# Audio-tower kernel on one Trainium2 core: one-hots by broadcast operands, small products moved around the token product, and five unused products in the prologue

## Chip, cores and metric

The kernel runs on one core of one Trainium2 chip. Time is device microseconds of one execution of the whole program, lower is better. The profile is of one execution; its times start at the first instruction.

## What is computed

Three layers over an input of 32 sequences of 125 frames with 23 features.

```python
# 1. token layer: windows of 5 frames, a product, relu, batch norm over all 32*121 rows
y = relu(einsum('blf,of->blo', patches, W) + b)
h = (y - mean) * rsqrt(var + eps) * gamma + beta
# 2. attention, 8 heads of 16, with a bias on each column (key position)
src, tgt = edge_index[0], edge_index[1]            # 8192 edges, targets 0..511
valid = (src >= 0) & (src < n) & (tgt >= 0) & (tgt < n)
last = full(n, -1).at[where(valid, tgt, 0)].max(where(valid, arange(8192), -1))
col_bias = where(last >= 0, (edge_attr @ eb_w.T + eb_b)[max(last, 0)], 0)
scores = q @ k.T / sqrt(16) + col_bias.T
h = h + softmax(scores) @ v @ o_w.T + o_b          # q, k, v from layernorm(h)
# 3. feed-forward: each row goes to one of 8 experts, gated by softmax over its one choice
h = h + W2[e] @ relu(W1[e] @ layernorm(h) + b1[e]) + b2[e]
```

The column bias needs, for each of the 121 positions, the **last** edge that points at it.

## The kernel before

The program is written by hand: each engine has its own list of instructions, in the order in which it is written, and semaphores join them. SyncE issues loads, TensorE (PE) does the products and transposes, ScalarE (ACT) and VectorE (DVE) copy and reduce, GpSimd (POOL) issues gathers and scatters and does the small norms. After the prologue a loop of 38 steps runs the attention of the 32 sequences as a pipeline, the first 11 expert tiles come in at its end, and 27 further tiles follow.

The change lies in the **prologue**, which goes from the first instruction to the first `scores` product (its products are written at line 1071). In it:

- PE transposes the input windows (`patches(0)` to `patches(7)`, L991) into PSUM; ACT copies each into `patT` (L461, the last piece L462) and counts `a_pat`. PE also transposes the weights of q, k and v (L1015), centres the router weights (L1021) and turns the bias rows of q and k into columns (L1037, one-column products; ACT copies them into `qk_col`, L550 and L551).
- DVE makes `key` (target plus 1, or 0) from the edges. PE transposes it, DVE copies it to `keyT`, and then writes 64 **one-hots** (L656, `target1h`, which lies in the memory of the weights `W1_sb` and so is called W_sb in the profile): one for each of 64 edge columns, 128 x 121, 1 where the key is the position. Eight at a time they count `a_1h`.
- PE multiplies each one-hot with powers of two (`edge_bits`, L999, 8 output columns each). The 64 results fill one PSUM bank, `bits`, from whose values DVE finds the last edge of each position. `edge_bits(c)` does eight of them. Four calls stand ahead of the token product, four behind it.
- The **token product** (L1030): eight products of 484 columns. It waits for `a_pat` 9. ACT applies relu (L468), DVE takes batch statistics (L660) and their aggregate (L662), POOL the inverse root (L371), DVE the scale and shift `bn_ac` (L668 to L670).
- The **index chain** on DVE: `col_hit` (L675, which waits for all `edge_bits`), `found` (L677) and six more steps up to `last_i` (L686). POOL then gathers the attributes of the last edges (`attr`, L374). POOL's next work is the first layer norm, `norm1(0)` (L380, L384, L388, L390), which makes `xn`.
- ACT makes `h0T` (L483) from the batch-normed tokens; PE turns it (`transpose_h0`, L1044), ACT copies it to `h0k` (L490) and sums squares. PE makes `owX` and the output bias (L1089, L1093, L1094), transposes `xn` (L1050), projects to k and q (L1055, 242 columns), and turns the padded column bias (L1103). ACT copies to `qT` (L502), DVE to `kT` (L723), and the scores begin.

The f32 products and their weight loads stand twice in the counts of the profile (two passes each).

## Time and profile before

| | |
|---|---|
| median of 3 runs | 287.25 us |
| the 3 runs | 287.51, 287.25, 284.8 us |
| the profiled execution | 285.12 us |
| its span, first to last instruction | 283.3 us |
| first `scores` product in it | 39.62 us after the start |
| granted TensorE clock, mean | 0.953 of full |
| busy, share of the span | PE 84%, PEld 71%, DVE 66%, ACT 59%, POOL 50% |

The profiled execution is 2.1 us under the median of the runs, and its span leaves 1.8 us of it outside. The granted clock is the share of 2.4 GHz that TensorE was given; 0.5 is its lower level, 1.2 GHz.

### The profile page before, as it was taken

To read this page: it belongs to the slowest core of one execution; us is meant where nothing else is said; L and a number is where in the kernel's file an instruction comes from. 1 tells how busy PE (TensorE), PEld (TensorE's weight loads), DVE (VectorE), ACT (ScalarE), POOL (GpSimd) and SP (SyncE) were. 2 spreads that over 40 slices of the span, in tenths; PEclk is the share of its full clock that TensorE was granted. 3 is DMA by queue.
4 is the path that set the end of the run, shared out by engine and by line. 5 is a ranking of instruction groups with operands and counts; after the bars stand their busy time and mean duration, and the time that the engine had idled before them with its cause. 6 is when DMAs were issued, how large, how long until landed. Compare 5 with 4: busy or idle time off the path is not lost.

```text
span 283.3 us, 9039 instructions
## 1 busy us (share of the span) xinstructions
PE 237.1 (84%) x2843; PEld 200.3 (71%) x2843; DVE 186.2 (66%) x762; ACT 166.6 (59%) x405; POOL 141.6 (50%) x259
## 2 busy tenths in 40 slices
PE   3898697999899898998998987795677899999960
PEld 3746475678677686776876765584566899999950
DVE  3898445576877878778787787647555456556630
ACT  3854334676766667666675564744553577777720
POOL 8101613345347666577666743515776345545550
PEclk9977579999999999999999999979999999999995
DMA  3100199200001101011110112531223553342000
GB/s 114 43 38 0 38 353 300 61 0 3 2 2 38 30 29 39 18 39 27 32 38 20 35 39 55 135 75 42 75 74 91 139 143 96 96 114 69 26 3 0
DMA packets 14461, 18.20 MB, mean 64 GB/s; under 512 B 3991, under 2 KB 10555, under 8 KB 14416
## 3 DMA queue, kind: packets, MB, share of 16 engines
q1 hardware_dynamic: 10976, 11.23, 14.3%
q0 software_dynamic: 3296, 6.00, 7.2%
q8 instruction: 24, 0.39, 0.6%
q10 hardware_dynamic: 144, 0.41, 0.4%
q14 instruction: 21, 0.17, 0.2%
HBM read 10.58 MB, written 7.54 MB: 64 GB/s over the span
## 4 chain that ended last, share of the span: by engine, by line
PE 59%; DVE 19%; issue 10%; POOL 4%; ACT 2%; DVEq 2%; DMA 1%; ACTq 0%; POOLq 0%
PE psS L1152 9%; PE psB L1055 9%; PE psS L1071 6%; PE psU L1139 4%; PE psO L1139 4%; PE psS L1081 4%; DVE kT L723 3%; PE psB L1139 3%; DVE nmax L858 2%; PE psU L1227 2%; PE psO L1244 2%; PE psB L1061 2%; PE psO L1199 2%; PE psB L1044 2%; PE psU L1205 2%
## 5 line engine op out<-in xcount | busy, mean ns | idle before, releaser
L419 POOL DMA_INDIRECT out<-y_out,sidx x38 | 37.0, 974 | 31.6 <-DVE y_out L825 24.6
L858 DVE TENSOR_REDUCE nmax<-psS 121x8 f32<-121x968 f32 x32 | 37.3, 1165 | 16.9 <-PE psS L1081 14.5
L833 DVE TENSOR_SCALAR hT<-psS,b1T 128x128 f32<-128x128 f32 x76 | 23.2, 347 | 32.0 <-PE psS L1152 29.3
L1152 PE MATMUL psS<-xgT,W_tile 128*128 128x128 f32 x304 | 41.1, 279 | 0.0
L412 POOL DMA_INDIRECT region_d<-rows,pos x32 | 34.7, 1084 | 9.2 <-issue 8.9
L588 ACT ACTIVATE PT<-psS 121x968 f32<-121x968 f32 x32 | 31.3, 978 | 13.0 <-DVE nmax L858 10.6
L1152 PEld LDWEIGHTS psS<-xgT,W_tile 128*128 128x128 f32 x304 | 37.9, 196 | 0.0
L537 ACT ACTIVATE hT<-psS,b1T 128x128 f32<-128x128 f32 x76 | 23.8, 363 | 12.9 <-PE psS L1152 12.9
L1071 PE MATMUL psS<-kT,qT 32*121 32x121 f32 x512 | 22.3, 287 | 7.2 <-DVE kT L723 6.4
L518 ACT ACTIVATE W_tile<-W_sb 128x512 f32 x38 | 24.0, 630 | 7.1 <-issue 4.9
L1071 PEld LDWEIGHTS psS<-kT,qT 32*121 32x121 f32 x512 | 16.9, 179 | 15.1 <-issue 8.2
L401 POOL TENSOR_SCALAR var<-ss 121x1 f32<-121x1 f32 x32 | 6.4, 201 | 37.5 <-DVE sq L909 31.1
L575 ACT ACTIVATE oT<-psO 128x121 f32<-128x121 f32 x32 | 8.7, 273 | 26.6 <-PE psO L1199 26.6
L875 DVE TENSOR_TENSOR qm<-qT,psU 128x242 f32<-128x242 f32 x32 | 13.0, 408 | 14.1 <-PE psU L1231 13.3
L1244 PE MATMUL psO<-PT,V 121*32 121x121 f32 x512 | 20.2, 276 | 0.0
L1139 PE MATMUL psB<-W_sb,hT 128*128 x88 | 12.8, 288 | 8.6 <-DVE y_out L825 7.0
L1081 PE MATMUL psS<-qm,kT 32*121 32x121 f32 x512 | 19.8, 264 | 0.0
L406 POOL TENSOR_TENSOR rs<-var,minus_half 121x1 f32<-121x1 f32 x32 | 18.0, 562 | 2.7
L1139 PEld LDWEIGHTS psB<-W_sb,hT 128*128 128x128 f32 x88 | 10.7, 192 | 10.5 <-issue 10.5
L1055 PE MATMUL psB<-xT,qwT 128*128 128x242 f32 x64 | 18.0, 406 | 0.0
L1055 PE MATMUL psB<-xT,kwT 128*128 128x242 f32 x64 | 16.8, 387 | 0.6 <-ACT xT L497 0.6
L1081 PEld LDWEIGHTS psS<-qm,kT 32*121 32x121 f32 x512 | 17.0, 181 | 0.1
(255 smaller groups left out, 566.7 us busy)
## 6 DMA issues: line engine op xcount, KB each, us to landing
xg<-region_d SPq DMA_DIRECT2D x38, 129.0 KB, 2.2
W_sb<-in_L_ffn_W SPq DMA_DIRECT2D x1, 2048.0 KB, 9.6
region_d<-pads SPq DMA_DIRECT2D x1, 1032.0 KB, 7.0
out<-y_out,sidx POOLq DMA_INDIRECT x38, 2.7
b_bc<-in_L_ffn_b SPq DMA_DIRECT2D x1, 512.0 KB, 5.3
region_d<-rows,pos POOLq DMA_INDIRECT x32, 3.0
xs<-in_x ACTq DMA_DIRECT2D x1, 402.5 KB, 3.7
edge_i<-in_L_attn_edge_index SPq DMA_DIRECT2D x1, 64.0 KB, 3.9
```

Source lines behind the costliest of these rows:

```text
L412: pool.indirect_dma_start(region_d, bass.IndirectOffsetOnAxis(pos[0:L, b:b + 1], 0), rows[0:L, b, E:E + ROW], None, bounds_check=E * CAP - ...
L419: pool.indirect_dma_start(out, bass.IndirectOffsetOnAxis(sidx[:, s:s + 1], 0), y_out[:, u, :], None, bounds_check=N - 1, oob_is_err=False) ...
L518: act.activation(W1_tile[:, s % 2, :], W1_sb[:, bass.ds(e * F, F)], ACT.Identity).then_inc(f_w1, 1)
L537: ins = act.activation(hT[:, s % 2, c * 128:(c + 1) * 128], psS[:, s % 2, c * 128:(c + 1) * 128], ACT.Relu, bias=b1T[:, bass.ds(e * FC + c ...
L588: act.activation(PT[0:L, (t - 1) % 2, :, :, :], score_half(1), ACT.Exp).then_inc(s_exp, 1)
L858: dve.tensor_reduce(nmax[0:L, :].rearrange("p (j c) -> p j c", c=HB)[:, :, HD + 1:HD + 3], score_half(0), AX.X, ALU.max, negate=True).then ...
L1055: return pe.matmul(bank[:, g * PL:(g + 1) * PL], w[:, g * 128:(g + 1) * 128], xT[:, p % 2, :], start=True, stop=True)
L1071: ins = pe.matmul(psS[0:L, j, a * 128:a * 128 + L], qT[rws, p % 2, a, n0:n0 + L], kT[rws, p % 2, a, n0:n0 + L], start=True, stop=True)
L1081: ins = pe.matmul(psS[0:L, j, 256 + a * 128:256 + a * 128 + L], kT[rws, p % 2, a, n0:n0 + L], qm[rws, a, :], start=True, stop=True)
L1139: ins = pe.matmul(tile_out(s), hT[:, s % 2, c * 128:(c + 1) * 128], W2_sb[:, bass.ds(e * F + c * D, D)], start=(c == 0), stop=(c == FC - 1))
L1152: ins = pe.matmul(psS[:, c // 2 * 2 + s % 2, c % 2 * 128:(c % 2 + 1) * 128], W1_tile[:, s % 2, c * 128:(c + 1) * 128], xgT[:, s % 2, :], s ...
L1244: ins = pe.matmul(psO[j * HB:(j + 1) * HB, a * 128:a * 128 + L], V[0:L, (t - 2) // 2 % 2, t % 2, a * HG + j, :], PT[0:L, t % 2, j, a, :], ...
```

## The change

All of it is in the prologue.

- `keyT` becomes bf16, and the 64 one-hot instructions become 8, each comparing 8 edge columns at once (128 x 968): the iota is repeated along the columns, the key along the positions.
- PE: `patches(5)` to `(7)` now stand ahead of the weight transposes. The one-column products for the q and k bias stand ahead of the edge products and write into another bank; ACT copies them ahead of the first `h0T`. Two `edge_bits` calls stand ahead of the token product and six behind it (four and four before).
- DVE: `col_hit` stands ahead of the three `bn_ac` steps, and still waits for the last `edge_bits`.
- PE: five products whose result nobody reads (`idle_product`, 115 rows, 512 columns, f32): two ahead of `transpose_h0(0)`, two ahead of `transpose_h0(1)`, one ahead of the transpose of `xn`.

```diff
-        keyT = sb("keyT", [128, EF])
+        keyT = sb("keyT", [128, EF], BF16)
@@ ACT
             act.wait_ge(a_wrc, 1)
             act.activation(idX[:, 0:E], banks[1][:, 384:384 + E], ACT.Identity).then_inc(a_wts, 1)
+            act.wait_ge(a_bias, 1)
+            act.activation(qk_col[:, 0:2], banks[1][:, 392:394], ACT.Identity, scale=0.25).then_inc(a_wts, 1)
+            act.activation(qk_col[:, 2:4], banks[1][:, 394:396], ACT.Identity).then_inc(a_wts, 1)
...
             batch_norm(0)
-            act.wait_ge(a_bias, 1)
-            act.activation(qk_col[:, 0:2], banks[5][:, 0:2], ACT.Identity, scale=0.25).then_inc(a_wts, 1)
-            act.activation(qk_col[:, 2:4], banks[5][:, 2:4], ACT.Identity).then_inc(a_wts, 1)
             h0_copy(0, banks[6])
@@ DVE
             for c in range(8):
-                for f in range(8 * c, 8 * c + 8):
-                    ins = dve.tensor_scalar(target1h[:, f, :], slot_iota[:, 1:L + 1], keyT[:, f:f + 1], None, ALU.is_equal)
-                ins.then_inc(a_1h, 1)
+                dve.tensor_tensor(target1h[:, 8 * c:8 * c + 8, :],
+                                  slot_iota[:, 1:L + 1].unsqueeze(1).to_broadcast([128, 8, L]),
+                                  keyT[:, 8 * c:8 * c + 8].unsqueeze(2).to_broadcast([128, 8, L]),
+                                  ALU.is_equal).then_inc(a_1h, 1)
...
+            bits = banks[2][0:L, 0:EF * EG]
+            dve.wait_ge(a_bits, 8)
+            dve.wait_ge(s_colio, 1)
+            link(dve.scalar_tensor_tensor(out=col_hit[0:L, :], in0=bits, scalar=0.0, in1=col_iota[0:L, :],
+                                          op0=ALU.is_gt, op1=ALU.mult))
             dve.wait_ge(a_rstd, 1)
...
-            bits = banks[2][0:L, 0:EF * EG]
-            dve.wait_ge(a_bits, 8)
-            dve.wait_ge(s_colio, 1)
-            link(dve.scalar_tensor_tensor(out=col_hit[0:L, :], in0=bits, scalar=0.0, in1=col_iota[0:L, :],
-                                          op0=ALU.is_gt, op1=ALU.mult))
@@ PE
+            for t in range(5, 8):
+                patches(t)
             pe.wait_ge(l_proj, 64)
...
-            for t in range(5, 8):
-                patches(t)
...
+            pe.wait_ge(l_qkb, 32)
+            for n in range(4):
+                ins = pe.matmul(banks[1][:, 392 + n:393 + n], qk_row[0:1, n // 2, n % 2 * 128:n % 2 * 128 + 128],
+                                ident[0:1, 0:1], start=True, stop=True)
+            ins.then_inc(a_bias, 1)
...
-            for c in range(4):
+            for c in range(2):
                 edge_bits(c)
...
-            for c in range(4, 8):
+            for c in range(2, 8):
                 edge_bits(c)
-            pe.wait_ge(a_relu, 3)
-            pe.wait_ge(l_qkb, 32)
...
+            def idle_product(n):
+
+                for _ in range(n):
+                    pe.matmul(banks[0][:, 0:512], ident[0:CTX * DI, :], patT[0:CTX * DI, 0:512], start=True, stop=True)
...
             pe.wait_ge(a_wts, 5)
+            idle_product(2)
             transpose_h0(0, banks[6])
+            idle_product(2)
             transpose_h0(1, banks[7])
...
+            idle_product(1)
             transpose_xn(0, banks[1])
```

Below, L999, L1030 and so on are the lines of before; the changed kernel has the same instructions at L1000, L1036, L1056 (the unused products), L1060 and L1111.

**PE around the token product.** Before, ahead of it and behind it:

```order
L1015 MATMUL psS<-ident,proj_in 128x128 x3
L991 MATMUL psS<-ident,xs 115x128 x8
L991 MATMUL psO<-ident,xs 115x128 x3
L1021 MATMUL psS<-Wr_sb,idX 128x8
L999 MATMUL psS<-power_bf,W_sb 121x8 x32
L1030 MATMUL psS<-patT,tokWT 128x484
...
L1030 MATMUL psO<-patT,tokWT 128x484
L999 MATMUL psS<-power_bf,W_sb 121x8 x32
L1037 MATMUL psU<-ident,qk_row 128x1 x4
L1044 MATMUL psB<-idX,h0T 121x137 x4
```

After the change, the same place:

```order
L992 MATMUL psO<-ident,xs 115x128 x3
L1018 MATMUL psS<-ident,proj_in 128x128 x3
L1022 MATMUL psS<-Wr_sb,idX 128x8
L1025 MATMUL psS<-ident,qk_row 128x1 x4
L1000 MATMUL psS<-power_bf,W_sb 121x8 x16
L1036 MATMUL psS<-patT,tokWT 128x484
...
L1036 MATMUL psO<-patT,tokWT 128x484
L1000 MATMUL psS<-power_bf,W_sb 121x8 x48
L1056 MATMUL psS<-patT,ident 128x512 x2
L1044 MATMUL psB<-idX,h0T 121x137 x2
L1056 MATMUL psS<-patT,ident 128x512 x2
L1044 MATMUL psB<-idX,h0T 121x137 x2
```

Sixteen edge products have moved behind the token product, the bias columns ahead of it, and four unused products stand between the last edge products and the second pair of turned token blocks.

**DVE between the batch statistics and the index chain.** Before:

```order
L656 TENSOR_SCALAR W_sb<-slot_iota,keyT 128x121 x64
L660 BN_STATS bn_st<-yT 128x6 x8
L662 BN_AGGR bn_mv<-bn_st 128x2
L664 COPY vb_mat<-col 128x128
L665 COPY ob_mat<-col 128x128
L668 TENSOR_TENSOR bn_ac<-bn_r,col 128x1
L669 TENSOR_TENSOR bn_r<-bn_mv,bn_ac 128x1
L670 TENSOR_TENSOR bn_ac<-col,bn_r 128x1
L675 SCALAR_TENSOR_TENSOR W_sb<-psS,col_iota 121x512
L677 TENSOR_REDUCE found<-W_sb 121x1
```

After the change:

```order
L655 TENSOR_TENSOR W_sb<-slot_iota,keyT 128x968 x8
L661 BN_STATS bn_st<-yT 128x6 x8
L663 BN_AGGR bn_mv<-bn_st 128x2
L665 COPY vb_mat<-col 128x128
L666 COPY ob_mat<-col 128x128
L670 SCALAR_TENSOR_TENSOR W_sb<-psS,col_iota 121x512
L674 TENSOR_TENSOR bn_ac<-bn_r,col 128x1
L675 TENSOR_TENSOR bn_r<-bn_mv,bn_ac 128x1
L676 TENSOR_TENSOR bn_ac<-col,bn_r 128x1
L678 TENSOR_REDUCE found<-W_sb 121x1
```

The first step of the index chain now stands ahead of the three steps that ACT's `h0T` waits for, and the one-hots are 8 instructions.

## Rows read from the trace of the kernel before

**Rows 1.** The page: the granted clock in 40 slices of 7.08 us.

```profile
PEclk9977579999999999999999999979999999999995
```

**Rows 2.** The chain that ended last, in order of time: start, length, work.

```profile
8.46 5.16 DVE W_sb L656 x32
...
13.67 0.61 PE psS L999 x8
14.28 1.47 PE psS L1030 x2
...
25.35 0.17 DVE bn_ac L668
...
25.81 0.70 DVE W_sb L675
...
26.54 0.70 DVE found L677
...
28.81 0.17 DVE last_i L686
...
30.05 1.37 POOL attr L374
...
32.98 0.36 POOL xn L390
...
33.39 0.68 PE psS L1050 x2
...
34.61 1.95 PE psB L1055 x4
36.56 0.40 PE psU L1103 x2
36.96 1.61 PE psB L1055 x4
...
39.62 0.70 PE psS L1071 x16
```

**Rows 3.** Timeline of ACT and PE: start, length, work, operands, count.

```profile
12.98 0.29 ACT L462 ACTIVATE patT<-psO 115x32 f32<-115x32 f32 x1
...
18.35 1.79 PE L1030 MATMUL psB<-patT,tokWT 115*128 115x484 f32 x4
...
22.41 1.92 PE L999 MATMUL psS<-power_bf,W_sb 128*121 128x8 bf16 x32
...
26.66 1.24 PE L1044 MATMUL psB<-idX,h0T 128*121 128x137 f32 x4 [0.96 <-ACT qk_col L551]
...
28.97 0.57 ACT L483 ACTIVATE h0T<-yT,bn_ac 128x242 f32<-128x242 f32 x1
...
29.60 1.27 PE L1044 MATMUL psB<-idX,h0T 128*121 128x137 f32 x4 [1.70 <-ACT h0T L483]
...
40.25 0.43 PE L1050 MATMUL psO<-ident,xn 121*128 121x121 f32 x2
...
41.75 0.99 PE L1055 MATMUL psB<-xT,qwT 128*128 128x242 f32 x4
```

**Rows 4.** Busy time by stretch: PE, PEld, DVE, ACT, POOL, granted clock, DMA, GB/s.

```profile
14.60:17.80 3.20, 3.20 (x5) 1.35 (x4) 3.20 (x21) 1.07 (x2) 0.00 (x0) 0.50 0.07 27
...
22.40:24.40 2.00, 2.00 (x35) 1.97 (x33) 1.72 (x5) 1.30 (x6) 0.00 (x0) 1.00 0.00 0
...
24.80:28.00 3.20, 2.14 (x9) 1.75 (x8) 2.52 (x7) 0.77 (x4) 0.51 (x1) 0.50 0.00 0
...
34.60:38.20 3.60, 3.59 (x10) 3.02 (x11) 1.32 (x4) 0.00 (x0) 1.96 (x4) 0.50 0.95 320
...
185.00:188.60 3.60, 3.60 (x32) 3.30 (x30) 0.90 (x5) 1.53 (x4) 0.00 (x0) 0.53 0.48 108
```

**Rows 5.** DVE's groups by shape: line, operands, shapes, count, busy us, mean ns, idle before.

```profile
L761 DVE TENSOR_TENSOR oh_bf<-rank,top 121x32 bf16<-121x32 f32 x7 | 1.4, 206 | 0.2
...
L761 DVE TENSOR_TENSOR oh_bf<-rank,top 121x16 bf16<-121x16 f32 x2 | 0.3, 175 | 0.1
```

More of the change, by code:

```diff
@@ L1031, in _ @@
                           start=True, stop=True).then_inc(a_y, 1)
-            for c in range(4, 8):
+            for c in range(2, 8):
                 edge_bits(c)
-            pe.wait_ge(a_relu, 3)
-            pe.wait_ge(l_qkb, 32)
-            for n in range(4):
-                ins = pe.matmul(banks[5][:, n:n + 1], qk_row[0:1, n // 2, n % 2 * 128:n % 2 * 128 + 128],
-                                ident[0:1, 0:1], start=True, stop=True)
-            ins.then_inc(a_bias, 1)
             def transpose_h0(p, bank):
```

## Prediction

> **What bounds the kernel now.** I read the granted clock of the page first, then the chain of waits in order of time, then the stretches by busy time, then the timeline of each engine in the prologue. Only the prologue is changed, so the question is when the first scores product starts: 39.62 us now [rows 2]. From there on the loop has the same instructions in the same order, and what is saved before it is carried to the end unless the clock takes it back.
>
> The clock line has a 7 in two slices, then 5 and 7, between 14 and 42 us, and is near full after that [rows 1]: TensorE runs much of the prologue at its lower level of 1.2 GHz. The chain names five parts up to 39.62 us [rows 2]. DVE writes one-hots and PE waits for them until the token product can start at 14.28. The product, relu and statistics follow. The index chain on DVE starts only behind the three `bn_ac` steps, at 25.81, and ends with `last_i` at 28.98. POOL gathers `attr` and then makes `xn`, ready at 33.34. Last come the transposes of `xn`, the two projections and the bias on PE: 0.68, 1.95, 0.40 and 1.61 us, all at the lower clock (0.50 from 34.6 to 38.2, [rows 4]).
>
> **The change, part by part.** *Start of the token product.* Ahead of it PE now needs two groups of one-hots, not four. An old one-hot comes every 0.161 us (5.16 us for 32, [rows 2]). A new instruction writes 968 elements. No row has this shape. The nearest has the same form, one operand repeated along each dimension and bf16 out: 32 elements in 206 ns, 16 in 175 ns [rows 5], 1.9 ns an element at worst. From those I take about 1.1 us for 968 elements if it goes at one element a cycle like the other DVE rows, such as the 0.70 us for 512 of `found` [rows 2], and 2.0 us as the dear end. So two groups are there at 8.46 + 2.2 = 10.7 us, at worst 12.5, and all eight at 17.3, at worst 24.5. What is late next is ACT: its last copy to `patT` ends at 12.98 + 0.29 = 13.27 [rows 3], and the product waits for that. The sixteen edge products left ahead of it (0.06 us each, 1.92 us for 32, [rows 3]) and the four bias columns fit between about 10.7 and 13.3 us; if the two bias loads land late or those columns are slow, up to 0.5 us of the gain is lost. The product starts at 13.33 in place of 14.28, and everything up to the inverse root comes 0.95 us earlier. The new one-hots end at 17.3, when only one or two batches wait for their statistics, and that backlog is gone before the last batch. With `patches(5)` to `(7)` ahead of the weight transposes nothing changes for ACT, which copies without a gap; the weight copies have a later use.
>
> *Edge products behind it.* There are 48 and not 32: 48 x 0.06 = 2.88 us. They used to start at 22.41 and end at 24.33; now they start at 21.46 and end at 24.34. So `bits` is complete no earlier than before. The gain of the first part stops here.
>
> *Order on DVE.* `col_hit` waits for those edge products, to 24.4, and takes 0.70, to 25.1. Queued behind it are the three `bn_ac` steps, whose input is there from 25.35 - 0.95 = 24.4. They start at 25.1, 0.25 earlier than before and not 0.95, and ACT's `h0T` waits for them. `found` starts behind them at 25.7 in place of 26.54 [rows 2]: the index chain, the gather and `xn` come 0.85 us earlier, `xn` at 32.5. This is the part of the gain that survives on POOL, which works through gather and norm without waiting for the squares.
>
> *Bias columns.* ACT's two small copies leave the place between `h0T` and `h0_copy(0)`, where PE's product already covered them: nothing.
>
> *Five unused products.* Four passes of 484 columns take 1.79 us at the upper level, with the drain of the last in it [rows 3], so about 0.41 us each, and twice that at the lower. So 512 columns take 0.43 or 0.86 us a pass, and a product (two passes) 0.86 or 1.71 us. At 24.35 PE starts the first pair. In the trace the clock falls at about 24.8, while PE is busy without a gap with 8-column products [rows 4]; I take the same here. That pair then ends at about 27.3, where `h0T` has been ready since 26.3. `transpose_h0(0)` runs to 28.4, and not to 27.9 [rows 3]: 0.5 us late. But PE has then been busy for 3.9 us with broad products. In the trace the clock came back at about 17.9 behind broad products from 14.3 on, and again at about 38.4 behind the projections that began at 34.6 (0.50 in both stretches, [rows 4]). So I take it to be back by 28.3. The second pair fills the wait that was 1.70 us long [rows 3], to 30.1, just when the second `h0T` is ready (29.54 + 0.5). `transpose_h0(1)` and the output bias follow at the upper clock, to about 32.1, and the fifth product to about 33.0. `xn` has been ready since 32.5, so PE is what is late now: the transposes of `xn` start at 33.0 and not 33.39, 0.4 us earlier.
>
> *Projections at the upper clock.* The transposes take 0.43 and not 0.68, the first projection 0.99 and not 1.95 [rows 2, 3], the bias 0.20 and not 0.40 and the second projection 0.80 and not 1.61 by the ratio of the levels: 0.25 + 0.96 + 0.20 + 0.81 = 2.2 us. DVE's column bias is no later than the first projection's end, since its input comes 0.7 us earlier with the gather.
>
> **Sum**: 0.4 + 2.2 = 2.6 us less. The profiled execution took 285.12 us, which makes 282.5; against the median, which is 2.1 us higher, 287.25 - 2.6 = **284.6 us**. As two of the three runs took some 2.3 us more than the profiled one, and what I can see that differs between runs is where the clock falls, either of the two levels can be met.
>
> **Rivals.** *The clock never falls in the prologue's middle.* The broad products begin 0.45 us before the fall of the old trace; if they keep the upper level, the pairs cost 1.7 us each inside waits and PE is ready before `xn`. Then 0.85 + 2.2 = 3.05 us are saved: 284.2 us. Against it stands that PE was busy for all 2.00 of the 2.00 us before the fall [rows 4], and there are now more 8-column products, not fewer. The Trainium skill (TensorE: Matmul & The Clock Gate, § HAM oscillation) lets the clock fall in idle gaps between bursts; by that it would stay up here, and the trace disagrees with it, since the clock fell behind 2.00 busy us of 2.00. Chance 0.14.
>
> *Unused products at the lower clock: slower.* If the clock is not back when the second pair starts, both pairs cost 3.4 us: `transpose_h0(0)` ends at 29.0, the second pair at 32.4, `transpose_h0(1)` at 33.7 against 30.87 [rows 3], the rest at 35.8 as slow as before, the fifth product at 37.5. PE reaches `xn` 4.1 us later than at 33.39 and still projects at the lower clock: 287.25 + 4.1 = 291.4 us. It decides from the point at which the clock returns later than about 31 us. For it: products of 137 columns at the lower level did not bring the clock back from 26.66 to 34. Against it: they had waits of 0.96 and 1.70 us between them, and there would be none. Chance 0.06.
>
> *The clock returns and falls again before the projections.* Between 31 and 34 us PE waits for `owX`, for `xn` and for ACT's copy. Then only the 0.4 us are left: 286.9 us. The fifth product fills the longest of these waits. Chance 0.12.
>
> *The gain is changed by the clock later.* From 185 to 188.6 the clock was at 0.53 while PE was busy throughout [rows 4]; such a spell costs up to 1.7 us. With everything moved by 2.6 us, it can vanish (283.0) or another come (286.3). Chance 0.14, half each.
>
> *The new one-hots at the dear end, or dearer.* At 2.0 us they end at 24.5, and eight statistics of 484 elements stand behind them, some 0.66 us each by the rate of `found`: ready at 29.8, when even `bn_ac` had begun at 25.35 [rows 2]; at least 4.5 us slower, 291.8. From about 1.3 us an instruction on it begins to cost. The shorter rows of [rows 5] carry mostly fixed cost, so I hold it unlikely. Chance 0.02.
>
> **How the numbers follow.** The forecast has the other 0.52. The range must hold eight in ten: the slow rivals (0.08) stay out, the two quick cases and the case of 0.4 us are in, and beyond them there is the 2.3 us between single runs of before: from 282.0 to 287.2 us. A measurement of this kernel tells about 1% from no change, 2.9 us, so the bound is 284.4, just beside the forecast. Somewhat under half of the forecast's 0.52, all but a little of the first rival and half of the clock's case lie beyond it: 0.45. Slower by over 1% are the two slow rivals: 0.08. Within 1%: 0.47.
>
> **What the profile after would show.** The token product starting at 13.3 to 13.5, behind ACT's last `patT` copy; eight one-hots of 1.1 us; `col_hit` waiting for PE until about 24.4; `found` at 25.7; the granted clock low for about 3.5 us from 24 to 28 and full from there through 38; the transposes of `xn` behind an unused product at 33.0; the projections at 0.99 us; the first scores at about 37.0. I am wrong if the clock stays low past 31, if the one-hots take over 1.3 us, or if the scores start at 37 and the end does not move.

## Result, and the profile after

| | before | after |
|---|---|---|
| median of 6 runs | 287.25 us | 282.96 us |
| lowest to highest | 284.80 to 288.04 | 281.65 to 284.21 |
| profiled execution, its span | 285.12, 283.3 us | 282.78, 281.1 us |
| mean granted clock of the profiled execution | 0.953 | 0.966 |

The ratio of the times is 0.9891, with a 95% interval of 0.9850 to 0.9931: 1.1% faster by that, 1.5% by the two medians. The ratio and its interval leave disturbed runs out, here and below, the medians don't. The forecast was 284.6 us, with a range of 282.0 to 287.2; the measured median lies inside it, 1.6 us below the forecast.

The page of the changed kernel, the granted clock in 40 slices of 7.03 us:

```profile
PEclk9997999999999999999999999995979999999995
```

In place of the 7, 7, 5, 7 of before [rows 1] there is one 7 in the prologue, at 21 to 28 us. Later on there is a 5 and a 7 (190 to 197 and 204 to 211 us), where before had a single 7.

The chain that ended last, start, length, work, to be read against [rows 2]:

```profile
13.62 0.07 ACT patT L462
13.72 1.08 PE psS L1036 x2
...
20.49 2.78 PE psS L1000 x48
23.27 3.37 PE psS L1056 x4
26.64 0.47 PE psB L1044 x4
27.11 1.72 PE psS L1056 x4
28.83 0.71 PE psB L1044 x4
...
30.91 0.86 PE psS L1056 x2
31.77 0.22 PE psS L1050 x2
...
32.53 1.05 PE psB L1060 x4
33.59 0.21 PE psU L1111 x2
33.80 0.84 PE psB L1060 x4
...
35.68 0.70 PE psS L1076 x16
```

The token product now starts behind ACT's last `patT` copy and no longer behind one-hots. DVE's index chain and POOL's `xn` have left the chain: from the edge products (L1000) on, it is PE with its unused products (L1056), then the transposes of `xn` (L1050) and the projections (L1060) at 1.05 and 0.84 us, where before they took 1.95 and 1.61. The first scores start at 35.68 us, 3.94 earlier.

The timeline of DVE and POOL, start, length, work, operands, count:

```profile
8.40 8.70 DVE L655 TENSOR_TENSOR W_sb<-slot_iota,keyT 128x968 bf16<-128x968 bf16 x8
...
23.31 0.69 DVE L670 SCALAR_TENSOR_TENSOR W_sb<-psS,col_iota 121x512 f32<-121x512 f32 x1 [0.81 <-PE psS L1000]
...
30.91 0.37 POOL L390 TENSOR_SCALAR xn<-h0k,rs 121x128 f32<-121x128 f32 x1
```

A new one-hot is 8.70 / 8 = 1.09 us. `xn` is ready at 30.91 + 0.37 = 31.28, and PE turns to it only at 31.61.

Busy time by stretch, columns as in [rows 4] (the eighth is the granted clock):

```profile
14.60:17.80 3.20, 3.20 (x9) 1.52 (x8) 3.20 (x5) 2.52 (x4) 0.00 (x0) 1.00 0.07 23
22.40:24.40 2.00, 2.00 (x16) 1.48 (x15) 1.11 (x4) 0.00 (x0) 0.75 (x2) 0.61 0.00 0
24.80:28.00 3.20, 3.20 (x10) 1.70 (x9) 1.91 (x8) 1.23 (x5) 0.01 (x1) 0.77 0.00 0
34.60:38.20 3.60, 2.99 (x34) 2.48 (x33) 1.88 (x3) 2.74 (x7) 0.04 (x1) 1.00 1.03 388
...
188.00:195.00 7.00, 5.56 (x32) 5.05 (x31) 4.16 (x24) 1.99 (x6) 4.12 (x7) 0.65 0.16 46
195.00:202.00 7.00, 4.31 (x30) 3.83 (x28) 3.28 (x18) 3.77 (x10) 4.82 (x5) 0.86 0.26 73
202.00:209.00 7.00, 6.70 (x44) 6.57 (x44) 3.14 (x18) 3.21 (x10) 5.38 (x6) 0.76 0.24 71
```

The first row is the token product: 1.00 (2.4 GHz), where before stood 0.50 (1.2 GHz). The second and third give the one spell at the lower level: 0.61 of 2.00 us is 1.56 us at half clock, so it began at about 22.8, and 0.77 of 3.20 us is 1.47 us, so it ended at about 26.3. The projections run at 1.00. The last three rows lie in the expert tiles; in the same three stretches before had 0.96, 1.00 and 1.00, and its one late spell lay just ahead of them (185.2 to 188.6, see [rows 4]).

**Where the time went.** The first scores come 3.94 us earlier, and the last `exp` of the attention loop starts at 175.59 and not 179.59, 4.00 us earlier: the loop carries all of it. The last `exp`, before and after:

```profile
179.59 0.98 ACT L588 ACTIVATE PT<-psS 121x968 f32<-121x968 f32 x1
```

```profile
175.59 0.98 ACT L588 ACTIVATE PT<-psS 121x968 f32<-121x968 f32 x1
```

The profiled execution as a whole is 2.34 us shorter. The rest went in the expert tiles. The group of the 304 products with W of the experts, before and after (line, shapes, count, busy us, mean ns, idle before):

```profile
L1152 PE MATMUL psS<-xgT,W_tile 128*128 128x128 f32 x304 | 41.1, 279 | 0.0
```

```profile
L1160 PE MATMUL psS<-xgT,W_tile 128*128 128x128 f32 x304 | 43.4, 289 | 0.0
```

The same instructions took 2.3 us more, by the clock that the three stretches show. This need not be the change's doing: in before_again, a second profile of the kernel before on a slower chip (A, see below), they took longest of all runs, and the clock stood at 0.94, 0.57 and 0.92 in the three stretches.

```profile
L1152 PE MATMUL psS<-xgT,W_tile 128*128 128x128 f32 x304 | 45.2, 298 | 0.0
```

The changed kernel on that chip, after_again, took 44.2 us for them. There the first scores come 38.74 - 35.85 = 2.89 us earlier and the whole span is 291.3 - 288.3 = 3.0 us shorter, so nothing is lost behind the prologue. The profile of before above was a quick execution (285.12 us against a median of 287.25), with a high clock in the expert tiles.

### The profile page after: what moved, and what is told of

It reads as the page before. It is cut to its first block, busy times and chain, and to the rows that moved or that the text cites. A ratio compares the mean times of both kernels' runs of the same rounds, so it can differ in the third digit from the quotient of the medians.

```text
span 281.1 us, 9002 instructions
## 1 busy us (share of the span) xinstructions
PE 239.8 (85%) x2853; PEld 202.1 (72%) x2853; DVE 184.2 (66%) x706; ACT 166.9 (59%) x405; POOL 141.9 (51%) x259
## 4 chain that ended last, share of the span: by engine, by line
PE 65%; DVE 15%; issue 10%; ACT 3%; POOL 2%; DMA 1%; DVEq 1%; ACTq 0%; POOLq 0%
PE psS L1160 11%; PE psB L1060 8%; PE psS L1076 6%; PE psU L1147 4%; PE psO L1147 4%; PE psS L1086 4%; DVE kT L724 4%; PE psB L1147 4%; DVE nmax L859 3%; PE psB L1044 2%; PE psU L1235 2%; PE psS L1056 2%; PE psO L1207 2%; PE psB L1066 2%; PE psO L1252 2%
## 5 line engine op out<-in xcount | busy, mean ns | idle before, releaser
L834 DVE TENSOR_SCALAR hT<-psS,b1T 128x128 f32<-128x128 f32 x76 | 23.2, 346 | 34.1 <-PE psS L1160 31.6
L1160 PE MATMUL psS<-xgT,W_tile 128*128 128x128 f32 x304 | 43.4, 289 | 0.0
L1160 PEld LDWEIGHTS psS<-xgT,W_tile 128*128 128x128 f32 x304 | 39.9, 204 | 0.0
L540 ACT ACTIVATE hT<-psS,b1T 128x128 f32<-128x128 f32 x76 | 23.8, 363 | 14.2 <-PE psS L1160 14.1
L1147 PE MATMUL psB<-W_sb,hT 128*128 x88 | 13.6, 302 | 7.7 <-DVE y_out L826 6.0
L1147 PEld LDWEIGHTS psB<-W_sb,hT 128*128 128x128 f32 x88 | 11.7, 207 | 9.6 <-issue 9.6
L1060 PE MATMUL psB<-xT,qwT 128*128 128x242 f32 x64 | 17.2, 391 | 0.0
L528 ACT ACTIVATE xgT<-psB 128x128 f32<-128x128 f32 x38 | 10.0, 263 | 11.7 <-PE psB L1136 11.6
```

The lines of the kernel that those rows point to most:

```text
L540: ins = act.activation(hT[:, s % 2, c * 128:(c + 1) * 128], psS[:, s % 2, c * 128:(c + 1) * 128], ACT.Relu, bias=b1T[:, bass.ds(e * FC + c ...
L1060: return pe.matmul(bank[:, g * PL:(g + 1) * PL], w[:, g * 128:(g + 1) * 128], xT[:, p % 2, :], start=True, stop=True)
L1147: ins = pe.matmul(tile_out(s), hT[:, s % 2, c * 128:(c + 1) * 128], W2_sb[:, bass.ds(e * F + c * D, D)], start=(c == 0), stop=(c == FC - 1))
L1160: ins = pe.matmul(psS[:, c // 2 * 2 + s % 2, c % 2 * 128:(c % 2 + 1) * 128], W1_tile[:, s % 2, c * 128:(c + 1) * 128], xgT[:, s % 2, :], s ...
```

## Experiments

The first eight of the table ran on one chip (A), the last four on another (B). On A the kernel before took 293.2 us, on B 286.2. So each ratio is against the kernel before on its own chip. In traces the start of the first scores is compared, which the chip hardly touches (38.74 us for the kernel before on A, and 39.62 in the profile above, where it took 287.25 in all).

| kernel | median us | before us | ratio, 95% interval | first scores | clock at the lower level, 12 to 42 us |
|---|---|---|---|---|---|
| no_unused | 292.26 | 293.2 | 0.9967 (0.9939 to 0.9995) | 38.74 | 14.2 to 17.7, 24.5 to 38.1 |
| unused_only | 290.75 | 293.2 | 0.9937 (0.9911 to 0.9964) | 37.74 | 23.2 to 30.0 |
| onehot_only | 292.26 | 293.2 | 0.9953 (0.9923 to 0.9983) | 38.97 | 14.9 to 18.3, 25.1 to 38.8 |
| fill_tiles | 295.70 | 293.2 | 1.0074 (1.0049 to 1.0098) | 35.09 | none (42.5 to 46.0) |
| after_again | 290.04 | 293.24 | 0.9904 (0.9873 to 0.9936) | 35.85 | 23.1 to 26.5 |
| before_again | 293.16 | 293.24 | 0.9996 (0.9975 to 1.0018) | 38.74 | 23.6 to 37.2 |
| colhit_back | 290.48 | 293.24 | 0.9909 (0.9881 to 0.9938) | 36.94 | 14.9 to 18.3, 25.1 to 28.5 |
| split_4_4 | 290.52 | 293.24 | 0.9915 (0.9888 to 0.9942) | 36.08 | 14.8 to 18.2 |
| old_onehots | 281.88 | 286.23 | 0.9861 (0.9808 to 0.9915) | 36.12 | none |
| narrow_unused | 288.67 | 286.23 | 1.0012 (0.9969 to 1.0055) | 42.05 | 22.6 to 43.1 |
| drop_first | 282.76 | 286.23 | 0.9886 (0.9840 to 0.9932) | 35.71 | 25.5 to 28.9 |
| drop_last | 282.41 | 286.23 | 0.9834 (0.9774 to 0.9895) | 36.40 | 32.4 to 35.9 |

The last two columns are of one profiled execution each; the ends of the clock's spells are worked out from stretches of 1 us, in the way shown above.

**The changed kernel without the five unused products.**

```diff
-            idle_product(2)
             transpose_h0(0, banks[6])
-            idle_product(2)
             transpose_h0(1, banks[7])
...
-            idle_product(1)
             transpose_xn(0, banks[1])
```

> The changed kernel without its five unused products. Theory (the clock carries most of the gain): the clock stays at its lower level from the middle of the prologue to the projections, as before the change; the first scores product starts at about 37.5 to 38.5 us instead of 35.7, and the time is about 2 us over the changed kernel, 285 us. Rival (the unused products only fill waits, the reordering carries the gain): first scores at 35.5 to 36, time within 0.5 us of the changed kernel, 283 us.

Measured: 0.9967, against 0.9904 for the changed kernel on the same chip. The medians are 2.2 us apart. The clock by stretch:

```profile
24.80:28.00 3.20, 1.24 (x4) 0.94 (x4) 2.85 (x12) 0.91 (x2) 0.00 (x0) 0.50 0.00 0
28.00:30.00 2.00, 0.67 (x3) 0.67 (x4) 0.00 (x0) 1.25 (x6) 0.95 (x1) 0.50 0.00 0
30.00:32.00 2.00, 1.56 (x7) 1.27 (x7) 0.72 (x5) 0.88 (x2) 1.73 (x4) 0.50 0.03 1
...
34.60:38.20 3.60, 3.60 (x13) 3.04 (x11) 1.26 (x3) 0.42 (x2) 1.71 (x4) 0.51 1.01 368
```

With waits in place of the products PE is busy for 0.67 to 1.56 us of each 2, the clock stays at 0.50, and the first projection takes 1.95 us (timeline: start, length, work):

```profile
33.70 1.95 PE L1060 MATMUL psB<-xT,kwT 128*128 128x242 f32 x4 [0.55 <-ACT xT L500]
```

From there to the first scores it is 38.74 - 33.70 = 5.04 us; in the changed kernel it is 35.68 - 32.53 = 3.15. That difference of 1.9 us is what the unused products bring, and it is most of the 2.89 us that the whole change brings to the first scores on this chip. The first scores of no_unused start no earlier than those of before_again (38.74 both), though it has all the other edits; but in no_unused the token product ran partly at the lower level, and in before_again it didn't.

**The kernel before with the unused products alone.**

```diff
+            idle_product(2)
             transpose_h0(0, banks[6])
+            idle_product(2)
             transpose_h0(1, banks[7])
...
+            idle_product(1)
             transpose_xn(0, banks[1])
```

> The kernel before plus the five unused products and nothing else of the change. Theory: the clock is back before the projections and they take 0.99 instead of 1.95 us; first scores at about 37.4 instead of 39.6, time about 285 us. Rival (without the reordering the first pair comes too late and delays the turned token blocks): first scores at 39 or later, time as before, 287 us.

Measured: 0.9937 (1.8 us); first scores at 37.74. The timeline of PE:

```profile
23.97 3.78 PE L1056 MATMUL psS<-patT,ident 115*128 115x512 f32 x4
...
28.46 2.67 PE L1056 MATMUL psS<-patT,ident 115*128 115x512 f32 x4
...
34.60 1.05 PE L1060 MATMUL psB<-xT,kwT 128*128 128x242 f32 x4 [0.55 <-ACT xT L497]
```

The first pair runs at the lower level (3.78 us for 4 passes, against 1.88 in the changed kernel's second pair), the clock returns in the second pair, at about 30, and holds through the projections. Left over for the other edits are 0.9937 - 0.9904, about 1 us, and as much by the other route, no_unused, 0.9 us. So in the totals the parts add up, within intervals of some 0.3% (0.9 us) each. The first scores alone come 1.0 us earlier than in before_again: the projections are quick, but PE takes up `xn` 0.85 us later (33.67 against 32.82), since the slow first pair stands in its way.

**The kernel before with the broadcast one-hots and the bf16 key alone.**

```diff
-                for f in range(8 * c, 8 * c + 8):
-                    ins = dve.tensor_scalar(target1h[:, f, :], slot_iota[:, 1:L + 1], keyT[:, f:f + 1], None, ALU.is_equal)
-                ins.then_inc(a_1h, 1)
+                dve.tensor_tensor(target1h[:, 8 * c:8 * c + 8, :],
+                                  slot_iota[:, 1:L + 1].unsqueeze(1).to_broadcast([128, 8, L]),
+                                  keyT[:, 8 * c:8 * c + 8].unsqueeze(2).to_broadcast([128, 8, L]),
+                                  ALU.is_equal).then_inc(a_1h, 1)
```

> The kernel before with the eight one-hot instructions and bf16 keys and nothing else. Theory: each takes 1.1 us instead of 8 x 0.16 = 1.29 us, so four groups are there after 4.35 us and not 5.16; the token product starts 0.7 us earlier, first scores 0.7 us earlier, time 286.4 us, which cannot be told from before. Rival (the one-hots are the bound of the whole stretch, and TensorE's waits for them cost clock too): first scores over 1.5 us earlier, time 285.5 us or less.

Measured: 0.9953, first scores at 38.97, and the token product starts at 13.44. So with faster one-hots the four groups ahead of the product are hardly late any more: PE still waits 0.46 us for the last of them, and the product starts 0.7 to 0.8 us earlier than in the kernel before (14.14 and, in before_again, 14.25).

**The changed kernel with the old one-hots.** Same edit, the other way round.

> The changed kernel with the 64 old one-hot instructions (f32 keys) and the new order. Theory: two groups need 2.6 us in place of 2.2, so the token product still starts behind ACT's last copy, at 13.2 to 13.8 us; the last one-hots end at 18.8 and not 17.0, and the batch statistics behind them catch up before the last one. First scores within 0.5 us of the changed kernel's 35.9, ratio to before 0.990 to 0.993: the broadcast one-hots are not needed once two groups stand ahead. Rival (DVE's later end holds the statistics up): first scores over 0.8 us later, ratio 0.994 or more.

Measured: 0.9861, below what was expected, with an interval that overlaps those of the changed kernel, at 0.9891 and 0.9904. The timeline of DVE:

```profile
8.37 10.38 DVE L656 TENSOR_SCALAR W_sb<-slot_iota,keyT 128x121 bf16<-128x121 bf16 x64
18.67 4.61 DVE L660 BATCH_NORM_STATS2 bn_st<-yT 128x6 f32<-128x484 f32 x8
```

The one-hots end at 18.75, not at 17.1, and the statistics that queue behind them without a gap end at 23.28. With only two groups ahead of the product, it starts at 13.37. So either the faster one-hots or the split of two and six takes the one-hots out of PE's way, and in the total the two together can't be told from one.

On DVE it is not so. The kernel to compare with is fill_tiles, whose prologue is that of the changed kernel and whose clock did not fall before 42 us either. Its statistics:

```profile
17.06 4.60 DVE L661 BATCH_NORM_STATS2 bn_st<-yT 128x6 f32<-128x484 f32 x8
```

They end at 21.66, 1.6 us earlier. `found` starts at 24.11 in fill_tiles and at 25.17 with the old one-hots, and PE's transposes of `xn`, which wait for POOL in both, follow (old_onehots, then fill_tiles):

```profile
31.99 0.42 PE L1049 MATMUL psS<-ident,xn 121*128 121x121 f32 x2 [0.67 <-POOL xn L390]
```

```profile
30.96 0.43 PE L1050 MATMUL psS<-ident,xn 121*128 121x121 f32 x2 [0.70 <-POOL xn L390]
```

The first scores start at 36.12 and 35.09. So at the same clock the old one-hots put them 1.03 us later, by the way that the rival of this run named (over 0.8 us). Each is one execution, and fill_tiles ran on the other chip; but drop_last, on the same chip as old_onehots, took up `xn` as early as fill_tiles, at 30.91, also waiting for POOL. In the total it doesn't show.

**Four groups ahead and four behind, with all else changed.**

```diff
-            for c in range(2):
+            for c in range(4):
                 edge_bits(c)
...
-            for c in range(2, 8):
+            for c in range(4, 8):
                 edge_bits(c)
```

> The changed kernel with four groups of edge products ahead of the token product and four behind it, as before the change. Theory: ACT's last copy at 13.2 to 13.7 us sets the start of the token product, the third and fourth groups need their one-hots only at 12.8 us and are done by 13.4, so the product starts 0 to 0.3 us later while sixteen edge products (0.96 us) no longer stand behind it: scores 0.3 to 0.9 us earlier, time 0.1 to 0.3% under the changed kernel. Rival (the groups ahead of it hold the product up): product start at 14 us or later and no gain.

Measured: 0.9915, product at 13.37, first scores at 36.08. For the start of the product this is the same conclusion from the other side. The gain that was expected over the changed kernel (first scores 0.3 to 0.9 us earlier) isn't seen, 36.08 against 35.85; but in this execution the token product ran partly at the lower level, so the first scores can't settle it.

**`col_hit` back behind the three `bn_ac` steps.**

```diff
-            link(dve.scalar_tensor_tensor(out=col_hit[0:L, :], ...))
             dve.wait_ge(a_rstd, 1)
...
             dve.tensor_tensor(bn_ac[:, 1:2], col3[:, 2:3], bn_r[:, 0:1], ALU.subtract).then_inc(a_ac, 1)
+            link(dve.scalar_tensor_tensor(out=col_hit[0:L, :], ...))
```

> The changed kernel with the first step of the index chain moved back behind the three steps of scale and shift on DVE. Theory: scale and shift come 0.7 us earlier (they no longer wait for the edge products), the index chain starts 0 to 0.2 us later; TensorE, not the layer norm, is what is late at the first transposes, so the first scores move by less than 0.4 us and the time is that of the changed kernel within 0.3%. Rival (the index chain sets the start of the loop): first scores 0.5 to 0.7 us later.

Measured: 0.9909, against 0.9904. Its first scores (36.94) belong to an execution of 294.03 us, far above its median, with the token product partly at the lower level, so they aren't held against the edit. The intervals are 0.3% to either side: if that order on DVE brings something, it is too little to be told here.

**The first pair left out; the fifth product left out.**

```diff
-            idle_product(2)
             transpose_h0(0, banks[6])
```

> The changed kernel without the first pair of unused products (three are left). Theory: the first turned token block no longer waits for the pair (0.7 to 0.9 us), but TensorE waits for it after the edge products, and the clock comes back only behind the second pair, at about 30 us or later; first scores at 36 to 37.5, ratio 0.991 to 0.995. Rival (the first pair only costs): first scores at 35.3 or earlier and a ratio under 0.990.

```diff
-            idle_product(1)
             transpose_xn(0, banks[1])
```

> The changed kernel without the fifth unused product. Theory: TensorE no longer comes 0.3 us late to the first layer norm, and the clock, back since 26 us, stays up: first scores 0.3 us earlier than the changed kernel's, ratio 0.989 to 0.991, not to be told from it. Rival (without it the clock falls again in the wait before the projections): granted clock 0.50 from 31 to 34 us, first scores 1.5 us or more later.

Measured: 0.9886 without the first pair, 0.9834 without the fifth product. Both intervals overlap that of the changed kernel (0.9850 to 0.9931), so neither is shown to be better. What was expected of the first (first scores at 36 to 37.5, the clock back at about 30 or later) did not come: 35.71 and 28.9. So the first pair isn't shown to be needed. The trace of the second tells what the fifth product guards against. Stretches and timeline of PE:

```profile
28.00:30.00 2.00, 0.93 (x7) 0.55 (x5) 1.00 (x6) 0.87 (x2) 1.84 (x3) 1.00 0.06 1
30.00:32.00 2.00, 0.54 (x3) 0.34 (x4) 1.56 (x5) 0.37 (x1) 1.75 (x6) 1.00 0.14 40
33.00:35.00 2.00, 2.00 (x7) 1.69 (x6) 1.21 (x3) 0.00 (x0) 1.13 (x3) 0.50 0.90 319
```

```profile
30.91 0.43 PE L1050 MATMUL psS<-ident,xn 121*128 121x121 f32 x2 [1.53 <-POOL xn L390]
31.89 1.42 PE L1060 MATMUL psB<-xT,kwT 128*128 128x242 f32 x4 [0.55 <-ACT xT L500]
```

PE is busy for 0.93 and 0.54 of 2 us while it waits for `xn`, and at about 32.4, in the first projection, the clock drops to 1.2 GHz: 1.42 us where it would be 1.05, and a second one of 1.83. PE took up `xn` 0.7 us earlier (30.91 against 31.61; 0.4 of it because `xn` was ready earlier, at 30.86) and had the first scores 0.7 us later (36.40 against 35.68). In the total this doesn't show.

**Narrow unused products: four of 8 columns for each one of 512.**

```diff
-                for _ in range(n):
-                    pe.matmul(banks[0][:, 0:512], ident[0:CTX * DI, :], patT[0:CTX * DI, 0:512], start=True, stop=True)
+                for _ in range(4 * n):
+                    pe.matmul(banks[0][:, 0:8], ident[0:CTX * DI, :], patT[0:CTX * DI, 0:8], start=True, stop=True)
```

> The changed kernel in which each unused product of 512 columns is replaced by four of 8 columns in the same place, which keep TensorE busy about as long at the upper clock (0.1 us a pass with its weight load). Theory (it takes broad products to bring the clock back; the clock fell behind products of 8 columns): the clock stays at its lower level from about 24 to 38 us, the projections take 1.95 us, first scores at 38 to 39, ratio 0.996 or more. Rival (any products will do, if TensorE does not wait): clock back by 31 us, first scores at 36 to 37, ratio 0.990 to 0.992.

Measured: 1.0012, and 1.0085 by the medians; all of the gain is gone. Stretches and timeline of PE:

```profile
24.80:28.00 3.20, 3.20 (x16) 3.20 (x16) 2.12 (x8) 0.59 (x1) 0.00 (x0) 0.50 0.00 0
28.00:30.00 2.00, 2.00 (x12) 2.00 (x11) 0.00 (x0) 1.58 (x6) 1.64 (x3) 0.50 0.00 0
30.00:32.00 2.00, 2.00 (x10) 2.00 (x11) 0.00 (x0) 0.00 (x0) 1.38 (x3) 0.50 0.04 1
```

```profile
23.34 3.56 PE L1056 MATMUL psS<-patT,ident 115*128 115x8 f32 x16
...
37.02 1.95 PE L1060 MATMUL psB<-xT,kwT 128*128 128x242 f32 x4 [0.56 <-ACT xT L500]
```

PE is busy for every microsecond from 24.8 to 32, and the granted clock stays at 0.50; in the changed kernel PE is just as busy in 24.8 to 28.0, with broad products, and the clock is back at 26.3. So in these two traces, with PE equally busy, the clock came back behind the broad products and not behind the narrow ones. The narrow ones also load weights all the time (PEld 3.20 of 3.20 us, 1.70 with the broad ones), and these runs don't tell the one difference from the other. The Trainium skill (TensorE: Matmul & The Clock Gate, § HAM oscillation) ties the fall of the clock to idle gaps between bursts. The trace of drop_last, where PE had waited before the fall, agrees with it in kind; this one and that of the changed kernel, where the clock fell at 22.8 behind 8-column products without a gap, do not.

This is also the mechanism of the rival "unused products at the lower clock": the clock isn't given back, and the transposes of `xn` start at 35.82, 4.3 us after `xn` is ready (31.48). Of its twelve runs nine took 287.1 to 290.1 us, and three took 285.1 to 285.5, at a mean granted clock of 0.960 where the slowest two had 0.937 and 0.943. I read them as runs in which the clock came back all the same, but of those there is no trace.

**Unused products in the expert tiles too**, to ask whether what is given back there can be had: three of 256 columns in each of tiles 1 to 10.

```diff
                 pe.wait_ge(f_hV, s + 1)
+                if 0 < s < NT1:
+                    for _ in range(3):
+                        pe.matmul(psS[:, s % 2, 256:512], ident[0:CTX * DI, :], patT[0:CTX * DI, 0:256], start=True, stop=True)
```

> The changed kernel with three more unused products of 256 columns in each of the expert tiles 1 to 10, behind the wait for the relu and ahead of the wait for the tile's sum. Theory (part of the prologue's gain is given back because the clock falls two or three times between 190 and 209 us, where TensorE waits for DVE's sums): with TensorE busy there the granted clock stays at 1.00 or falls once, and the time is 1 to 1.7 us under the changed kernel, 281.5 us. Rival (these waits hide the slow clock anyway, and 10 x 0.65 us of products stand in the way where there is no wait): time equal or up to 3 us over the changed kernel.

Measured: 1.0074, and the medians lie 5.7 us above after_again. The clock did what was wanted: 1.00 in three stretches where after_again had 0.67, 0.84 and 0.76. Stretches:

```profile
188.00:195.00 7.00, 5.05 (x35) 4.55 (x35) 5.14 (x28) 2.92 (x10) 3.18 (x5) 1.00 0.19 52
195.00:202.00 7.00, 6.02 (x46) 5.46 (x44) 2.45 (x14) 1.90 (x6) 4.72 (x5) 1.00 0.25 69
202.00:209.00 7.00, 4.52 (x34) 4.17 (x33) 1.58 (x9) 2.10 (x7) 4.75 (x5) 1.00 0.21 63
```

And the price, in the groups of this kernel and of after_again:

```profile
L1163 PE MATMUL psS<-xgT,W_tile 128*128 128x128 f32 x304 | 40.7, 278 | 0.0
...
L1144 PE MATMUL psS<-patT,ident 115*128 115x256 f32 x60 | 16.6, 415 | 6.8 <-issue 2.5 <-DVE hT L834 2.2 <-ACT hT L540 2.1
```

```profile
L1160 PE MATMUL psS<-xgT,W_tile 128*128 128x128 f32 x304 | 44.2, 293 | 0.0
```

The expert products got 3.5 us shorter, but PE spent 16.6 us on the unused ones. From the last `exp` to the end of the span it took 118.4 us and 112.4 without them, 6.0 us more. If all of the 3.5 us came through, 9.5 of the 16.6 us stood in front of products that were ready, and the other 7 filled waits. That is an estimate from these rows and wasn't tried by itself.

**The two kernels again**, on chip A.

> The changed kernel once more, beside the one before on the same chip as the runs that follow, so that both are read from traces of one chip. Theory: the saving is made in the prologue, by where the clock falls and returns there: first scores near 35 to 36 us, ratio to before 0.985 to 0.993. Rival (the ratio of the first measurement came from where the clock happened to fall later on): first scores as early, but a ratio near 1.

> The kernel before, taken once more with a profile. Theory: ratio 1.000 within 0.3%; first scores at 38.5 to 40.5 us by where the clock falls; on this chip the expert tiles at 200 to 215 us hold waits of some 6 us that the first profile did not have, in the kernel before as in the others. Rival: these waits are not in the kernel before, and the variants run so far have brought them in.

Measured: 0.9904 and 0.9996. The gain holds on a chip on which the kernel takes 6 us longer, 3.2 us there by the medians. In before_again the token product ran at 1.00, and its first scores began at 38.74: 0.9 us of the 3.94 are thus not the change's doing, but come with where the clock fell in the profiled run of before. PE's transposes of `xn`, in before_again and in after_again:

```profile
32.82 0.67 PE L1050 MATMUL psS<-ident,xn 121*128 121x121 f32 x2 [0.39 <-POOL xn L390]
```

```profile
31.78 0.37 PE L1050 MATMUL psS<-ident,xn 121*128 121x121 f32 x2
```

So of the 2.89 us on this chip 1.04 lie ahead of these transposes and 1.85 behind them.

**What varies between runs.** Each run has a mean granted clock on record. By a straight line through the six runs of the changed kernel the time falls by 1.6 us for each 0.01 of clock (281.65 us at 0.978, 284.21 at 0.967), through the twelve of narrow_unused by 2.3, through the twelve of after_again by 1.3 (289.05 at 0.971, 293.62 at 0.940); through the six of fill_tiles, which differ little in clock (0.964 to 0.972), by 0.6. So much of the spread of 3 to 5 us inside one kernel goes with how long the clock is low.

## Why the prediction was right, step by step

**Right in the main: what the unused products do.** From the transposes of `xn` to the first scores I had worked out 2.2 us less. Before it was 39.62 - 33.39 = 6.23 us, after 35.68 - 31.61 = 4.07: 2.16 less. On chip A, where the clock of before_again was back at 37.2 and so before the end of its second projection, it is 1.85. no_unused and unused_only show that it is these products that bring it.

**Right: the clock still falls behind 8-column products, and broad ones bring it back.** The first rival (it never falls) did not come about in the profiled run of the changed kernel. It did in three others that hold the same products, old_onehots, fill_tiles and split_4_4 (no spell between 18.2 and 42), so 0.14 was low. As the rival had it, PE is then ready before `xn`: in fill_tiles it waited 0.70 us for it. I had the spell at 24.8 to 28.3; it was 22.8 to 26.3.

**Right: PE becomes what is late.** I had PE 0.5 us behind `xn`; it was 31.61 - 31.28 = 0.33.

**Right in kind, off in size: the start of the token product.** Behind ACT's last `patT` copy, as forecast. But that copy itself ended at 13.67, and not 13.27: 13.72 in place of 13.33. In the other runs with two groups ahead it lay between 13.21 (no_unused) and 13.89 (after_again), so the forecast is inside what varies from one execution to the next.

**The term that was mis-sized: "transposes of `xn` 0.4 us earlier".** It measured 33.39 - 31.61 = 1.78 us. I let the token product take as long as before, at the lower level it had there from 14.5 to 17.9, and so had the last edge product end at 24.34, "no earlier than before". In the changed kernel's profile the product ran at 1.00 and the edge products ended at 23.27, 1.07 us earlier, and everything that hangs on `bits` with them: `found` at 24.50 in place of 25.7, `xn` at 31.28 in place of 32.5. That the product ran at 1.00 isn't the change's doing, since in before_again it did too. It varies: colhit_back, split_4_4, no_unused and onehot_only had 0.52 to 0.54 in 14.6 to 17.8 us. The text with the sum said that the clock's place differs between runs, but applied it only to the end and not to this product.

But measured against before_again, with the product at 1.00 on both sides, the term is still 1.04 us and not 0.4. There the statistics on DVE follow the one-hots without a gap and are what is late: they end at 23.39, and at 22.05 in after_again, 1.34 us earlier. The prediction weighed the faster one-hots for the start of the token product and asked only whether they would do harm to the statistics. It did not see that in an execution with a fast token product they bring the statistics forward.

**The other mis-sized term: nothing lost later.** The forecast let all that is saved arrive at the end; 3.94 came in and 2.34 was left in the profiled run. The rival on the later clock named the mechanism and its size of up to 1.7 us, and 1.6 us (3.94 - 2.34) is what was lost, with the spells at 190 to 207 and not at 185. Two errors, 1.3 us (3.94 - 2.6) too little and 1.6 too much, thus nearly cancelled: the profiled run gained 2.34, and the sum was 2.6. Of the first, 0.9 us came from where the clock fell in the profile of before. In the pair on chip A, where the clock fell about as much late in both (304 expert products in 45.2 and 44.2 us), 2.89 came in and 3.0 was left. By the medians the gain is 4.3 us (287.25 to 282.96) and on chip A 3.2, so 2.6 was somewhat low. That the profiled run comes this near to the sum is luck; the term of 2.2 us is not.

**Right: the price of the one-hots.** 1.09 us each against 1.1, done at 17.10 against 17.3. **Right, and worth little: `col_hit`.** It waited for PE as said, and the order of DVE can't be told from the old one in the total.

**The slower rival** was real as a mechanism: narrow_unused is the case in which the clock doesn't come back, and PE takes up `xn` at 35.82, 3.0 us later than in before_again. Its time can't be told from that of the kernel before (1.0012), where the rival had 4.1 us more. With 512 columns it did not occur in any trace here.

**Open.** Why the clock falls where it does in the expert tiles: in the three stretches PE is busy for 4.3 to 6.7 of 7 us in the changed kernel at 0.65 to 0.86, for 4.2 to 5.1 before at 0.96 to 1.00, and for 4.7 to 5.5 in before_again at 0.57 to 0.94. So it is open too whether the change has any part in it. Why chip A is slower: its traces of the kernel before and of the changed one alike have one wait of ACT and DVE of 3.4 to 5.0 us (ending at 213.1 in after_again, at 217.0 in before_again) whose cause lies outside what the trace shows, and the profiles of before and after above have none there.

## What to carry to other kernels

Where PE waits in short pieces ahead of a dense stretch and the granted clock there reads 0.50, fill these waits with broad products whose result nobody reads, and check in the trace that PE isn't late by more than the clock gives back: here 5 products turned 6.2 us of dense work into 4.1. Leave out one at a time, too: here the total did without the first pair, as far as it can be measured. Do it only where PE waits on others; in stretches where products are ready, the same filling cost 5.7 us. And judge such a change by several runs and by stretches, since one profiled execution differs from the next by where the clock falls, by 1 us in the prologue and 2 us later on.

## What the runs showed of the hardware that was not expected

- The granted clock fell (at 22.8 us in the changed kernel, at 22.6 in narrow_unused) and stayed at 0.50 (24.8 to 32 us of narrow_unused) while PE was busy without a gap, with products of 8 columns. Behind products of 512 columns that began at 23.3 it was back at 26.3 (changed kernel).
- A two-source DVE operation in bf16 whose one operand repeats a single element along the innermost dimension took 1.09 us for 968 elements, 1.12 ns each; the old one-hots, one-source with the key as a scalar, took 10.38 / 64 = 0.162 us for 121, 1.34 ns each with the fixed part. An estimate from the two, if both pay the same for an element: the broadcast saves a fixed part of 0.03 us for each of 56 instructions (10.38 - 8.70 = 1.68 us), and no more. The Trainium skill (Vector Engine (DVE) Microarchitecture Reference, § 5.1) has such an operand run one element at a time, where a row read again and again would run in pairs; the trace agrees with the first half, and no run here shows the second.
- The same program took 286.2 us on one chip and 293.2 on another, and the time on the slower one went in the expert tiles: from the start of the last `exp` to the end of the span before_again took 291.3 - 178.60 = 112.7 us, and the profile of before 283.3 - 179.59 = 103.7. Of these 9 us the expert products account for some 4 (45.2 against 41.1 us busy), by the lower granted clock of that execution, and the wait named above for 4 to 5; both are estimates from one profile each.
